# Softmax reciprocals turned onto rows by four transposes a unit, with GpSimd widening them; tail instructions re-ordered

## The reference

```
x = x + softmax(mask(LN(x) Wq^T (ctx Wk^T)^T / sqrt(32))) (ctx Wv^T) Wout^T   # 32 heads of 32, 8 key groups
x = x + LN(x) W_base^T + b + 0.5 * fourier(low-rank update)
x = x + fake_quant(LN(x)) @ fake_quant(ctx)                                  # per batch
# last layer: 4 streams of 256 features, xs = LN-free x viewed (4, 256)
logits = rmsnorm(x) @ [W_res; W_pre; W_post]^T + bases                        # 16 + 4 + 4 per token
H_res  = sinkhorn(logits_res, 50 iterations, tau 0.1)                         # 4 x 4 per token
x = x + mix(LN(x) streams by gate*H_res + (1-gate)*I) + outer((sum_n pre_n xs_n) W_branch, post)
```

## Time and profile before

| | |
|---|---|
| median of 3 runs | 1090.54 us (1089.51 to 1091.5) |
| the profiled execution | 1089.52 us, span of its instructions 1087.7 us |
| busy: PE, DVE, ACT, POOL | 1044.4, 846.0, 663.4, 76.9 us |
| stage B | about 203 to 714 us of the span |
| stage E | about 970 us to the end |

### The profile page before, as it was taken

The page is one execution under the profiler, slowest core; times in us unless marked ns, Lnnn a source line. Parts: engine busy times, 40 slices in busy tenths (PEclk is TensorE's granted clock), DMA queues, the critical chain, the costliest instruction groups (busy, mean ns, idle before and its releaser), DMA issues. The chain is left out here.

```text
span 1087.7 us, 21182 instructions
## 1 busy us (share of the span) xinstructions
PE 1044.4 (96%) x7664; PEld 791.1 (73%) x7664; DVE 846.0 (78%) x1876; ACT 663.4 (61%) x1126; POOL 76.9 (7%) x68
## 2 busy tenths in 40 slices
PE   8999999999999999999999999999999999969848
PEld 7878888777777777777777777776888886536527
DVE  5754444799999999999999999965764343879998
ACT  5322221598899888888988888852321123648617
POOL 0220012200000000000000000000002112410000
PEclk9999999999999999999999999999999999989969
DMA  8457878932133332113332311157314000000003
GB/s 334 169 200 274 275 248 251 342 85 50 37 67 72 72 68 72 48 30 72 72 72 68 72 43 36 50 214 255 118 58 169 0 1 1 1 1 1 1 0 155
DMA packets 55569, 112.97 MB, mean 104 GB/s; under 512 B 7724, under 2 KB 21164, under 8 KB 55388
## 3 DMA queue, kind: packets, MB, share of 16 engines
q1 hardware_dynamic: 55402, 112.10, 33.2%
q10 hardware_dynamic: 50, 0.16, 0.0%
q0 software_dynamic: 64, 0.00, 0.0%
HBM read 83.99 MB, written 27.26 MB: 102 GB/s over the span
## 5 line engine op out<-in xcount | busy, mean ns | idle before, releaser
L887 DVE CUSTOM_DVE_ANT_0 XS<-b_psS,b_mbias 128x1024 f32<-128x1024 f32 x256 | 311.0, 1215 | 0.6 <-PE b_psS L765 0.4
L842 ACT ACTIVATE XS<-XS,b_mins 128x1024 f32<-128x1024 f32 x256 | 295.9, 1156 | 10.8 <-DVE b_mins L887 10.2
L801 PEld LDWEIGHTS b_psT<-ident,XS 128*128 128x128 f32 x2048 | 229.2, 140 | 68.7 <-issue 50.5
L801 PE MATMUL b_psT<-ident,XS 128*128 128x128 f32 x2048 | 272.8, 276 | 1.7 <-ACT b_PT L850 1.7
L896 DVE COPY b_PT<-b_psT 128x512 f32<-128x512 f32 x256 | 176.9, 691 | 33.7 <-PE b_psT L801 32.2
L850 ACT COPY b_PT<-b_psT 128x512 f32<-128x512 f32 x256 | 149.7, 585 | 45.3 <-PE b_psT L801 37.3
L765 PE MATMUL b_psS<-XTh 128*128 128x512 f32 x512 | 156.1, 422 | 0.8 <-DVE b_mins L887 0.4
L779 PE MATMUL b_psO<-b_PT,XTh 128*32 128x256 f32 x1984 | 132.8, 385 | 0.0
L765 PEld LDWEIGHTS b_psS<-XTh 128*128 128x128 f32 x512 | 85.1, 189 | 18.9 <-DVE b_mins L887 8.2
L779 PEld LDWEIGHTS b_psO<-b_PT,XTh 128*32 128x32 f32 x1984 | 51.7, 109 | 42.1 <-issue 20.8
L416 ACT ACTIVATE a_oh<-a_psM 128x512 fp32r<-128x512 f32 x24 | 14.2, 596 | 81.6 <-PE a_psM L335 60.1
(11 more groups left out here) (265 smaller groups left out, 1586.7 us busy)
## 6 DMA issues: line engine op xcount, KB each, us to landing
XS<-in_ctx SPq DMA_DIRECT2D x16, 512.0 KB, 5.8
XTh<-QHd SPq DMA_DIRECT2D x32, 256.0 KB, 4.7
XTh<-QLd SPq DMA_DIRECT2D x32, 256.0 KB, 5.1
XS<-in_ctx_turned SPq DMA_DIRECT2D x8, 512.0 KB, 10.5
XS<-in_x SPq DMA_DIRECT2D x8, 512.0 KB, 11.9
a_wst<-in_L_xattn_w_q SPq DMA_DIRECT2D x8, 512.0 KB, 5.9
a_xn<-in_ctx_turned SPq DMA_DIRECT2D x8, 512.0 KB, 4.1
QHd<-a_oh SPq DMA_DIRECT2D x16, 256.0 KB, 5.6
```

The costliest lines, as they stand in the source:

```text
L801: last_t = pe.transpose(psT[:, kt, :], Pr[:, k % PR, kt * P:(kt + 1) * P], ident[:])
L842: act.activation(Pr[:, k % PR, :], Sc[:, k % 4, :], ACT.Exp, bias=mins[:, k % 4:k % 4 + 1], scale=-1.0, accum_out=sums[:, u, j:j + 1]).the ...
L887: dve.tensor_tensor_reduce(out=Sc[:, k % 4, :], in0=psS[:, k % 2, :], in1=mbias[:, qt, :], scale=1.0, scalar=3.4e38, op0=ALU.add, op1=ALU.min,
```

## The change

Four edits.

1. The spread. POOL multiplies the 16 reciprocals of each query row by a constant one, each repeated 32 times, into `wide` (128x512, `widen`); PE turns `wide` in four 128x128 transposes onto `psO`. `wide` and the constant lie in the buffer that held stage A's last stored keys, so POOL waits once for that store. `rec_ready` now counts two per unit, DVE's reciprocal and POOL's widening. The last unit is handled the same way; its widening is on POOL's list of stage B, and ACT waits for its spread before it writes its second operand buffer in stage C.
2. Stage D, DVE: `sum_logits(0)` moves from before `combine(7)` to behind the copy of the last turned tile. ACT: `keep_x(7)` moves ahead of the two square roots.
3. The gate's exponential moves from the head of stage E to the tail of stage D on ACT.
4. Stage E, DVE: the loops become 1 + 7*(1+3+3); the reciprocals `hinv` are taken after the first loop of seven instead of before all loops.

```diff
     def spread(self, pe, ident):
-        pe.wait_ge(self.rec_ready, BG)
+        pe.wait_ge(self.rec_ready, 2 * BG)
         pe.wait_ge(self.O_kept, BG)
         for qt in range(QT):
-            for h in range(HPG):
-                one = self.rec[:, 1, qt * HPG + h:qt * HPG + h + 1].to_broadcast([P, DH])
-                last = pe.matmul(self.psO[h * DH:(h + 1) * DH, 1, qt * P:(qt + 1) * P], one, ident[:],
-                                 start=True, stop=True)
+            last = pe.transpose(self.psO[:, 1, qt * P:(qt + 1) * P], self.wide[:, qt, :], ident[:])
         last.then_inc(self.spread_done, 1)
...
-                pe.wait_ge(rec_ready, bg + 1)
-                pe.wait_ge(O_kept, bg + 1)
+                pe.wait_ge(rec_ready, it * 4 + 2 * u)
+                pe.wait_ge(O_kept, it * 2 + u)
                 for qt in range(QT):
-                    for h in range(HPG):
-                        one = rec[:, u, qt * HPG + h:qt * HPG + h + 1].to_broadcast([P, DH])
-                        last = pe.matmul(psO[h * DH:(h + 1) * DH, u, qt * P:(qt + 1) * P], one, ident[:],
-                                         start=True, stop=True)
+                    last = pe.transpose(psO[:, 1 - u, qt * P:(qt + 1) * P], wide[:, qt, :], ident[:])
                 last.then_inc(spread, 1)
...
+            for u in range(2):
+                pool.wait_ge(hand.stored[u], 32 * (KT + B * KVT))
+            pool.memset(one, 1.0).then_inc(one_ready, 1)
+            pool.wait_ge(one_ready, 1)
+            def widen(it, u):
+                pool.wait_ge(rec_ready, it * 4 + (2 * u + 1))
+                pool.tensor_tensor(wide.rearrange("p t (h d) -> p (t h) d", d=DH),
+                                   rec[:, u, :].unsqueeze(2).to_broadcast([P, STEPS, DH]),
+                                   one.unsqueeze(2).to_broadcast([P, STEPS, DH]), ALU.mult).then_inc(rec_ready, 1)
+            with pool.Fori(0, BG // 2) as it:
+                for u in range(2):
+                    widen(it, u)
...
                     end.keep_O(act)
+            act.wait_ge(end.spread_done, BG)
             attention_hi(1)
...
             keep_x(NT - 2)
+            keep_x(NT - 1)
             std_q()
-            keep_x(NT - 1)
             keep_logits(1)
             keep_logits(2)
+            act.wait_ge(tail.par_in, 80)
+            act.activation(streams.gate_exp[:], tail.gt[:], ACT.Exp, scale=-1.0)
...
             for t in range(NT):
-                if t == NT - 1:
-                    sum_logits(0)
                 combine(t)
...
             dve.tensor_copy(xT[:, KT // 2:KT, slot(NT - 1)], psX(NT - 1)[:, KT // 2:KT, :]).then_inc(x_kept_low, 1)
+            sum_logits(0)
             token_factors()
...
-        PER_LOOP, LOOPS = 7, (4, 3)
+        PER_LOOP, LOOPS = 7, (1, 3, 3)
...
             col_step(1)
-            dve.wait_ge(soft_step, 3)
-            dve.wait_ge(gate_step, 2)
-            dve.reciprocal(hinv[:], sums[:]).then_inc(lg, 1)
...
             iterations(LOOPS[0], n)
+            dve.wait_ge(soft_step, 3)
+            dve.wait_ge(gate_step, 1)
+            dve.reciprocal(hinv[:], sums[:]).then_inc(lg, 1)
+            iterations(LOOPS[1], n)
```

More of the change, by code:

```diff
@@ L631, in __init__, with take @@
         self.stored = [sem(f"b_stored{u}") for u in range(2)]
-    def take(self, PT, Vs, rec, sums, Os, AOs, psO):
-        self.PT, self.Vs, self.rec, self.sums, self.Os, self.AOs, self.psO = PT, Vs, rec, sums, Os, AOs, psO
+    def take(self, PT, Vs, rec, wide, sums, Os, AOs, psO):
+        self.PT, self.Vs, self.rec, self.wide, self.sums, self.Os, self.AOs, self.psO = (
+            PT, Vs, rec, wide, sums, Os, AOs, psO)
     def weigh(self, pe):
@@ L703, in stage_b @@
         Qs, Ks, Vs, mk8 = hand.Qs, hand.Ks, hand.Vs, hand.mk8
+        wide = hand.oh[:, 0, :].bitcast(F32).rearrange("p (t n) -> p t n", t=QT)
+        one = hand.oh[:, 1, 0:1].bitcast(F32)
         Sc = hand.XS[:, 0:4, :]
@@ L710, in stage_b @@
         psO = stack.enter_context(nc.psum_tensor("b_psO", [P, 2, S], F32))
-        end.take(PT, Vs, rec, sums, Os, AOs, psO)
+        end.take(PT, Vs, rec, wide, sums, Os, AOs, psO)
         mbias_first = sem("b_mbias_first")
@@ L715, in stage_b @@
         waited = sem("b_waited")
+        one_ready = sem("b_one_ready")
         qkv_in = hand.qkv_in
@@ L782, in weigh, with spread_rec @@
                     last.then_inc(weighed, 1)
-            def spread_rec(bg, u):
-                pe.wait_ge(rec_ready, bg + 1)
-                pe.wait_ge(O_kept, bg + 1)
+            def spread_rec(it, u):
+                pe.wait_ge(rec_ready, it * 4 + 2 * u)
+                pe.wait_ge(O_kept, it * 2 + u)
                 for qt in range(QT):
-                    for h in range(HPG):
-                        one = rec[:, u, qt * HPG + h:qt * HPG + h + 1].to_broadcast([P, DH])
-                        last = pe.matmul(psO[h * DH:(h + 1) * DH, u, qt * P:(qt + 1) * P], one, ident[:],
-                                         start=True, stop=True)
+                    last = pe.transpose(psO[:, 1 - u, qt * P:(qt + 1) * P], wide[:, qt, :], ident[:])
                 last.then_inc(spread, 1)
@@ L818, in body @@
                     if j == UNIT + 2 and not (first and u == 0):
-                        spread_rec(it * 2 + (u - 1), 1 - u)
+                        spread_rec(it, u)
                     turn(it, k0 + 1, first)
@@ L840, in exponentials @@
                 if j == 0 and not first:
-                    act.wait_ge(rec_ready, it * 2 + (u - 1))
+                    act.wait_ge(rec_ready, it * 4 + (2 * u - 3))
                 act.activation(Pr[:, k % PR, :], Sc[:, k % 4, :], ACT.Exp, bias=mins[:, k % 4:k % 4 + 1], scale=-1.0,
@@ L1030, in __init__ @@
         self.rowterm = sb("rowterm", [P, NT])
+        self.gate_exp = sb("gate_exp", [P, 1])
         self.LG = sb("logits", [P, NT, TailLoads.NL])
@@ L1962, in _ @@
             pe.wait_ge(post_added, NT)
-            pe.wait_ge(sink_near, LOOPS[1])
+            pe.wait_ge(sink_near, LOOPS[2])
             for t in range(NT):
@@ L1980, in _ @@
         def _(act):
-            act.wait_ge(par_in, 80)
-            act.activation(sums[:, 2 * NT:2 * NT + 1], gt[:], ACT.Exp, scale=-1.0).then_inc(gate_step, 1)
             act.wait_ge(setup, 2)
@@ L2139, in _ @@
             n += 5 * CHAINS
-            iterations(LOOPS[1], n, sink_near)
+            iterations(LOOPS[2], n, sink_near)
             times(n, 3, ra, T, M)
@@ L2143, in _ @@
             dve.wait_ge(chain, n + (3 * CHAINS - 1))
-            dve.wait_ge(gate_step, 4)
+            dve.wait_ge(gate_step, 3)
             Hv = H[:]
@@ L2177, in _ @@
             pool.tensor_tensor(soft, soft, over_streams(mx[:]), ALU.subtract).then_inc(soft_step, 1)
-            pool.wait_ge(gate_step, 1)
-            pool.tensor_scalar(sums[:, 2 * NT:2 * NT + 1], sums[:, 2 * NT:2 * NT + 1], 1.0, None, ALU.add
+            pool.tensor_scalar(sums[:, 2 * NT:2 * NT + 1], streams.gate_exp[:], 1.0, None, ALU.add
                                ).then_inc(gate_step, 1)
@@ L2192, in _ @@
             pool.tensor_scalar(gt[:], gp, -1.0, 1.0, ALU.mult, ALU.add).then_inc(gate_step, 1)
-            pool.wait_ge(gate_step, 3)
+            pool.wait_ge(gate_step, 2)
             pool.wait_ge(setup, 4)
```

## The result

| | before | after |
| --- | --- | --- |
| median of 14 runs each | 1091.48 us | 1087.41 us |
| ratio | | 0.9965, 95% interval 0.9958 to 0.9973 |
| profiled execution (span) | 1089.52 (1087.7) us | 1085.42 (1083.6) us |

The change makes the kernel 3.8 us faster; the interval is 2.9 to 4.6. The sum on record was -6.6 us. The direction was right, the size was not, and the predicted range, 1081.3 to 1087.5, ends 0.1 us above the median of the changed kernel.

The account below looks back on a forecast made before the run. PE's instruction list was taken to bound stage B. Terms -6.6 + 1.3 + 0 - 0.4 - 0.2 - 0.7 summed to -6.6 us, giving 1082.9 or 1083.9; predicted 1083.7 us, 8-in-10 range 1081.3 to 1087.5.

Parts of the forecast that it names:

- The spread (-6.6): Stage B: four transposes per spread save PE 0.44 us a unit, 15 places, -6.6 us; ends -3.6 and -7.0.
- The widening inside the stage (0): Stage B: POOL's widening, taken as 1.3 us, is covered by some 20 us and does not slow DVE: 0.
- The rival of a held DVE: Stage B: POOL's widening holds DVE, 1.0 us a unit, +15 to the sum, 1099 us; chance 6%.
- that of lost clock in stage B: Stage B: transposes replacing matmuls lose PE clock; a twentieth at 1.2 GHz costs 25 us, 1109 us; chance 2%.
- The end of stage B (+1.3): Barrier before stage C: the last widening makes POOL arrive last, +1.3 us, from 0 to 2.4.
- The last spread in stage C (0): Stage C: PE gains 0.4 to 0.6 us but then waits longer for DVE: 0, other end -0.6.
- Stages D and E (-0.4, -0.2, -0.7): Earlier combine -0.4 us, gate and table load moved -0.2, `hinv` after one loop -0.7 (bounds -0.5 and -0.9).
- The clock rival: Stage E: PE's clock falls in a pause before the mixing, which begins at 1.2 GHz: +3, 1087 us; chance 6%.
- Stage E, start: Table load and gate exponential move into stage D; DVE's preparation then limits: -0.2 us, bounds 0 and -1.4.
- The ends 1082.2 and 1088.0: Whole-kernel times in us with the spread at -7.0 or -3.6 and the end of stage B at 0 or +2.4.

Follow-up runs that it names:

- experiment 5: The changed kernel without its new tile, the last widening moved behind the barrier into stage C: ratio 0.9923 to the kernel before, 8.4 us faster.
- 1: The kernel before with only a pad added, an unused tile of 4 bytes per partition ahead of the logits: ratio 1.0022, middle 2.4 us slower.
- experiment 2: The changed kernel with the gate's exponential written over the gate, so no new tile: ratio 0.9948 to the kernel before, 5.7 us faster.
- 3: The kernel before with only the new spread and its widening on POOL, no new tile: ratio 0.9975, 2.7 us faster.
- 6: The changed kernel without its new tile, measured a second time: ratio 0.9940 to the kernel before, 6.6 us faster.
- 8: The changed kernel with its new tile 64 bytes wide instead of 4: ratio 0.9961 to the kernel before.
- 13: The kernel before with only the new spread and its widening, measured again: ratio 0.9967, median 1088.21 us beside 1091.91 for the kernel before.
- 4: The kernel before with only the edits of stages D and E, no new tile: ratio 0.9981, 2.1 us faster.
- 7: The kernel before with a pad of 4 bytes per partition directly ahead of the second layer's weights `WEh`: ratio 1.0011.

## Why the prediction was wrong

**The spread (-6.6): right.** Measured -6.64 in the stretch from the first reciprocal to the last, 0.44 a unit. The condition I named for it, that the ACT and DVE waits of over 1 us behind a spread are what 0.44 come out of, is what the rows show: 0.67 and 0.63 are left.

**The widening inside the stage (0): right.** 1.04 us and not 1.3, hidden, and DVE's instructions kept their length, 1215 ns. The Trainium skill, "SBUF — State Buffer", section "Who interferes with whom", says that a DVE instruction with at most one input in SBUF, outside the two-port modes, does not contend with GpSimd; the trace agrees, also for the custom instruction that the page doesn't list, which reads PSUM and the mask in SBUF. The rival of a held DVE did not occur. Nor did that of lost clock in stage B: it stays at 1.00, at fewer matmuls.

**The end of stage B (+1.3): right mechanism, measured +1.14**, undone in experiment 5. The prediction has it that PE's spread needs the widening only 7 us later; that experiment made use of it.

**The last spread in stage C (0): off by half a microsecond.** From C's first matmul to `c_TS` it was 47.31 us on average in 11 traces with the spread and 46.82 in 7 without (the low clock behind the barrier taken out; standard errors 0.09 and 0.12). PE did get through the spread 0.75 us sooner and only waited longer, as I wrote. But DVE, which it waits for, was later. Its instruction behind a wait that the profile puts down to the DMA of the rows of x, before and then after:

```profile
746.43 1.23 DVE L1595 TENSOR_TENSOR c_Ll<-c_src,c_Lh 128x1024 fp32r<-128x1024 f32 x1 [3.45 <-DMA XR<-in_x]
742.18 1.23 DVE L1612 TENSOR_TENSOR c_Ll<-c_src,c_Lh 128x1024 fp32r<-128x1024 f32 x1 [4.53 <-DMA XR<-in_x]
```

It starts 31.8 us behind C's first matmul before and 32.4 after, though these DMAs were issued at nearly the same distance. It is 32.4 too in the trace of the pad alone, which has the old spread, so that the spread is not the only thing that moves it. Why is open; nothing was tried on it.

**Stages D and E (-0.4, -0.2, -0.7): -1.68 instead of -1.3.** Up to the first iteration the combine gives 0.60: 0.85 less the reduction's 0.48 would be 0.37, and 0.23 more are gained behind it. That these come from ACT's earlier copy, and with it PE's last logits, is argued and not shown; the prediction names the copy but gives it nothing in its sum. `hinv` gives 0.83, all of its wait and itself, and 1.07 up to the mixing, which is outside its bounds of -0.5 and -0.9; why is open. The gate and table give 0.13 up to the first iteration and nothing that shows at the mixing. PE's wait before the preloads is 4.93 us and not 6, so they have slack as worked out. The clock rival did not occur.

**The step that failed is "Stage E, start" (-0.2)**: it priced the table load and the exponential that move and not the tile that the edit adds, and so the sum has no term at all for the second layer. It is +1.66 us (experiments 1 and 2), the largest part of the 2.8 us between -6.6 and -3.8. With it and with +0.5 for stage C, the steady terms are -6.64 + 1.14 + 0.5 + 1.66 - 0.85 - 0.71 - 0.12 = -5.0 us.

**From -5.0 to the measured -3.8 and -3.3.** The intervals, 2.9 to 4.6 and 1.6 to 4.8, do not hold 5.0. I added up the steady terms for the other kernels in the same way. The seven comparisons of kernels with the late barrier (the changed kernel twice, 2, 3, 6, 8 and 13) all fall short of their sums, by 0.1 to 2.3 us and 1.3 on average. The four without it (1, 4, 5 and 7) miss theirs by +0.7, -0.4, -0.6 and -0.5, where plus is slower. This points to the late barrier, but comparisons on one chip share the runs of the kernel before. What the barrier adds through the clock, if 3 of 10 is its share, is an estimated 0.3 x (5.35 - 3.66) = 0.5 us. That it does so is not shown: 3 of 10 against 0 of 8 comes by chance in 15 of 100 cases. The last 0.7 or so stays open. Stage A and its clock scatter by more than that: the same code up to 203 us took from 203.07 to 207.10 in the traces.

**Smaller things in the prediction.** Most of PE's instructions in stage B are not transposes, as it says against the rival of the clock: from 240 to 700 us they are 1850 of some 4620 by number. So that row was weaker than it reads; the clock of 1.00 in the changed kernel is what decides. The 2.36 us that the widening was scaled from are called the time of a POOL instruction alone; that one ran beside DVE's clip. The ends 1082.2 and 1088.0 are counted from 1083.9 and not from the forecast of 1083.7, from which they would be 1082.0 and 1087.8. None of these changes the account.

## What to carry to other kernels

Before costing an edit, ask what it allocates: a tile placed ahead of others moves them, and a change of 32 bytes in the distance between the two operands of a product lengthened it by 1.6%; reuse a tile where one is free, as experiment 2 did, or look at the stretch again after adding one. An instruction that is hidden inside a loop needs a second look at the loop's last round, where a barrier has no cover: move it behind the barrier if its reader comes later. Compare traces by stretches between instructions that both have; where the clock is alike, most repeat to some hundredths of a microsecond where whole runs scatter by microseconds, and show a term of 1 us that medians can't.

## What was not expected of the hardware

- The time of a matmul on 128x512 depends on how far its moving and its stationary operand lie from each other in SBUF: on `WEh` with `c_Lh` a median of 388 ns at the old distance and 392 to 399 at the others tried, with 384 matmuls of the second layer taking 101.02 us, or 102.35 to 102.95. It repeats: 101.02 in all nine traces at the old distance, 102.68 to 102.74 in the five that are 32 bytes off it. Which distances are good, and what in the memory does it, was not found. The Trainium skill, "TensorE: Matmul & The Clock Gate", section "Step-by-step: what each phase is for", says that loading the next tile's weights does not take SBUF read bandwidth from the running matmul. The trace agrees that they overlap: from 825 to 900 us of the changed kernel PE was busy for 75.00 us with matmuls and for 61.08 with loads. Why a distance should then count is answered neither by the page nor by a run.
- PE's granted clock falls from 2.4 to 1.2 GHz in short pieces behind waits of PE in some executions and not in others of the same kernel: in the first 20 us (11 of 18 traces), behind the barrier of stage B (3 of 18; 64 matmuls 5.35 us instead of 3.66) and behind the wait for `c_TS` (3 of 18; +1.6 us).
- POOL's widening of 128x16 to 128x512 took 1.04 us as a product of two broadcast operands and 1.50 as a scalar operation on one (a single instruction, in experiment 5).
